# Half of each gated expert row split in SBUF and turned by DMA transposes, and the scaling of a quarter of the attention probabilities moved from ScalarE to GpSimd

## The reference, cut to what matters

```python
# attention, per sequence: q, k, v = x @ wq.T, ...; rope on q and k
w = jax.nn.softmax(jnp.einsum('bqh,bkh->bqk', q, k) / scale, axis=-1)
out = jnp.einsum('bqk,bkh->bqh', w, v)
...
for _ in range(LOOPS):                      # LOOPS = 2
    z_norm = _rmsnorm(z, norm_w)
    scores = jax.nn.softmax(z_norm @ router_w, axis=-1)
    topk_vals, topk_idx = jax.lax.top_k(scores, TOP_K)      # 2 of 8
    ...
    for e in range(E):                      # h = silu(x @ w1) * (x @ w3); h @ w2
        mixed = mixed + flat_cw[:, e:e + 1] * _swiglu(flat_z, w1[e], w3[e], w2[e])
    z = z + mixed.reshape(B, S, D)
```

## Time and profile before

| | |
|---|---|
| time, median of 3 runs | 1049.28 us (1046.91 to 1052.38) |
| the profiled execution | 1050.72 us, span 1049.0 us |
| granted TensorE clock | 0.989 |
| busy share of PE, DVE, ACT, POOL | 94%, 66%, 55%, 55% |
| instructions | 22711 |

### The profile page before, as it was taken

How to read it: one execution, slowest core, us unless ns; L and a number is a source line. 1 busy time by engine, 2 the same in 40 slices (tenths; PEclk the granted TensorE clock), 3 DMA queues, 4 the chain that set the end, 5 groups by cost and what they waited for, 6 DMA issues and landing times.

```text
span 1049.0 us, 22711 instructions
## 1 busy us (share of the span) xinstructions
PE 987.4 (94%) x7246; PEld 678.7 (65%) x7246; DVE 690.5 (66%) x1497; ACT 574.7 (55%) x1122; POOL 579.5 (55%) x755
## 2 busy tenths in 40 slices
PE   7999997989999899999999999999999999999991
PEld 5677776668888577665666765666755566666661
DVE  7889987999999454684435557535469433575557
ACT  4578786668888545433335565335574333333333
POOL 3356686866798755444443366443365544455435
PEclk9999999999999999999999999999999999999996
DMA  9921111000000234334346435338434433665573
GB/s 315 370 68 31 38 32 22 1 6 21 15 26 16 67 107 125 87 69 101 91 109 167 132 98 139 88 106 181 112 111 117 96 91 92 170 173 119 143 187 130
DMA packets 153818, 109.26 MB, mean 104 GB/s; under 512 B 100992, under 2 KB 140544, under 8 KB 153728
## 3 DMA queue, kind: packets, MB, share of 16 engines
q1 hardware_dynamic: 140096, 70.82, 26.5%
q0 software_dynamic: 13632, 37.24, 12.0%
HBM read 54.27 MB, written 31.20 MB: 81 GB/s over the span
## 4 chain that ended last, share of the span: by engine, by line
PE 69%; DVE 9%; POOL 7%; DMA 6%; ACT 4%; issue 3%; SPq 0%; another core or an unknown queue 0%; POOLq 0%; ACTq 0%; DVEq 0%
PE psum_s L930 32%; PE psum_o L2336 16%; PE psum_s L2325 6%; DMA arena<-arena 4%; PE psum_s L1758 3%; PE psum_t L1753 2%; PE psum_t L764 2%; PE psum_o L1804 2%; POOL arena L1057 2%; DVE arena L1489 1%; DMA arena<-in_rope 1%; PE psum_o L1799 1%; PE psum_o L1811 1%; PE psum_s L1735 1%; PE psum_t L2300 1%
## 5 line engine op out<-in xcount | busy, mean ns | idle before, releaser
L930 PE MATMUL psum_s<-w_all,arena 128*128 x1704 | 392.0, 380 | 4.6 <-issue 1.9
L1980 POOL DMA_INDIRECT token_rows<-arena,result_row_of_row x142 | 147.1, 1036 | 296.5 <-ACT arena L2089 291.2
L930 PEld LDWEIGHTS psum_s<-w_all,arena 128*128 128x128 f16 x1704 | 157.8, 98 | 185.2 <-issue 10.9
L2336 PE MATMUL psum_o<-w_all,arena 128*128 x1704 | 209.4, 273 | 9.1 <-DVE arena L2264 8.2
L915 DVE SCALAR_TENSOR_TENSOR arena<-psum_s,gate_scale,arena 128x512 f32<-128x512 f32 x142 | 106.5, 750 | 161.1 <-ACT arena L909 80.6
L2336 PEld LDWEIGHTS psum_o<-w_all,arena 128*128 128x128 f16 x1704 | 164.7, 98 | 54.1 <-issue 15.4
L2264 DVE TENSOR_TENSOR arena<-psum_s,arena 128x512 f16<-128x512 f32 x142 | 97.8, 689 | 132.3 <-ACT arena L2082 114.2
L2089 ACT ACTIVATE arena<-psum_o 128x256 f32<-128x256 f32 x142 | 54.3, 383 | 216.8 <-PE psum_o L2336 214.1
L891 POOL DMA_INDIRECT arena<-sorted_rows,token_of_row x142 | 139.9, 986 | 49.3 <-issue 40.2
L909 ACT ACTIVATE arena<-psum_s,silu_scale 128x512 f32<-128x512 f32 x142 | 97.6, 687 | 108.1 <-PE psum_s L930 56.6
L2082 ACT ACTIVATE arena<-psum_s 128x512 f16<-128x512 f32 x142 | 84.7, 597 | 33.1 <-PE psum_s L2325 22.9
(11 more groups left out here) (326 smaller groups left out, 1364.8 us busy)
## 6 DMA issues: line engine op xcount, KB each, us to landing
arena<-token_rows SPq DMA_DIRECT2D x64, 256.0 KB, 3.1
w_all<-in_L_ffn_w SPq DMA_DIRECT2D x24, 512.0 KB, 10.1
sorted_rows<-w_all SPq DMA_DIRECT2D x24, 256.0 KB
out<-x_sb SPq DMA_DIRECT2D x7, 512.0 KB, 3.1
arena<-arena SPq DMA_TRANSPOSE x172, 2.4
arena<-sorted_rows,token_of_row POOLq DMA_INDIRECT x142
token_rows<-arena,result_row_of_row POOLq DMA_INDIRECT x142
x_sb<-in_L_attn_x SPq DMA_DIRECT2D x1, 2048.0 KB, 14.8
```

The costliest lines, as they stand in the source:

```text
L930: last = nc.tensor.matmul(bank, e_xT[:, u, lx * DC + c, :], w_split[:, bass.ds(e * EW + at, FF)], start=(q == 0), stop=(q == 3 * DC - 1))
L1980: nc.gpsimd.indirect_dma_start(rows, bass.IndirectOffsetOnAxis(ap=targets[:, at : at + 1], axis=0), y_row[:, u, :], None).then_inc(s_sent[ ...
L2336: last = nc.tensor.matmul(psum_e, hT[:, lh, c, :], w_split[:, bass.ds(e * EW + at, D)], start=(q == 0), stop=(q == 3 * FC - 1))
```

## The change

It has two parts.

**Attention.** `quarter_hi` stands at the head of ScalarE's step, ahead of the copy of oT and of `p_copy(t-1, 1)`. The scaling of the quarter in place is no longer ScalarE's: GpSimd does it in `quarter_lo`, and then subtracts.

**Experts.** `turn_h` transposes only the first two of the four 128-column chunks, and `h_hi` and `h_lo` split only these. The other half of `h_row` is split in SBUF: `half_hi` on ScalarE (behind `beside`, ahead of `y_copy`) and `half_lo` on VectorE (right behind `gate`), each 128x256. SP turns the two with `turn_half`, two DMA transposes of 128x256 float16, ahead of everything else in its iteration. `outer` waits for them after its first six matmuls. To make room, `y_row` has two buffers and not three, `turn_rows` runs three tiles ahead, and `store_rows` is issued one iteration later.

```diff
+            if s:
+                dve.wait_ge(s_half_lo, s)          # in gate(s)
...
                 if l: sp.wait_ge(s_split_lo, t)
-                        sp.wait_ge(s_p_hi, 4 * t + 2)
+                        sp.wait_ge(s_quarter, t)
...
             def quarter_lo(t):
                 pool.wait_ge(s_quarter, t)
+                nc.gpsimd.tensor_scalar(probs[:, 0:512], probs[:, 0:512], P_SCALE, None, ALU.mult).then_inc(s_scaled, 1)
+                pool.wait_ge(s_scaled, t)
                 nc.gpsimd.tensor_tensor(probs_split[:, 1, :], probs[:, 0:512], probs_split[:, 0, :],
...
             def quarter_hi(t):
-                nc.scalar.activation(probs_split[:, 0, :], probs[:, 0:512], ACT.Copy, scale=P_SCALE).then_inc(s_p_hi, 1)
-                act.wait_ge(s_p_hi, 4 * t + 2)
-                nc.scalar.activation(probs[:, 0:512], probs[:, 0:512], ACT.Copy, scale=P_SCALE).then_inc(s_quarter, 1)
+                nc.scalar.activation(probs_split[:, 0, :], probs[:, 0:512], ACT.Copy, scale=P_SCALE).then_inc(s_quarter, 1)
...
+                if turn and quarter:
+                    quarter_hi(t - 1)              # head of step(t)
                 if turn and quarter:
-                    p_copy(t - 1, 1)
-                    quarter_hi(t - 1)
+                    p_copy(t - 1, 1, 2)
...
+            def turn_half(n):
+                for l, ready in enumerate((s_half_hi, s_half_lo)):
+                    sp.wait_ge(ready, n + 1)
+                    if n and l == 0:
+                        sp.wait_ge(s_e, n)
+                    sp.dma_start(hT[:, l, FC // 2 :, :], h_split[:, l, :], transpose=True).then_inc(s_half_T, 16)
             for k, plan in enumerate(plans):
                 for t in range(PASS[k]):
-                    turn_rows(sp, FIRST[k] + t + 2)
+                    n = FIRST[k] + t
+                    turn_half(n)
+                    if n == 0:
+                        turn_rows(sp, 2)
+                    turn_rows(sp, n + 3)
...
-                    if k < END and 0 <= t - plan.split - 1 < PAIRS:
-                        store_rows(k, t - plan.split - 1)
+                    if k < END and 0 <= t - plan.split - 2 < PAIRS:
+                        store_rows(k, t - plan.split - 2)
...
+            def half_hi(n):
+                act.wait_ge(s_h, n + 1)
+                if n:
+                    act.wait_ge(s_half_T, 32 * n)
+                nc.scalar.activation(h_split[:, 0, :], h_row[:, FF // 2 :], ACT.Copy).then_inc(s_half_hi, 1)
             def y_copy(n):
-                if n >= UNROLL:
-                    act.wait_ge(s_sent[u], 16 * (n // UNROLL))
+                if n >= 2:
+                    act.wait_ge(s_sent[(n - 2) % UNROLL], 16 * ((n - 2) // UNROLL + 1))
...
                     if k < END:
                         beside(k, plan, t)
+                    half_hi(n)
                     if n:
                         y_copy(n - 1)
...
+            def half_lo(n):
+                dve.wait_ge(s_half_hi, n + 1)
+                nc.vector.tensor_tensor(h_split[:, 1, :], h_row[:, FF // 2 :], h_split[:, 0, :], ALU.subtract).then_inc(s_half_lo, 1)
...
                     gate(dve, n)
+                    half_lo(n)
...
             def turn_h(n):
                 pe.wait_ge(s_h, n + 1)
-                for c in range(FC):
+                for c in range(FC // 2):
...
                 for q, (c, lh, lw) in enumerate([(c, a, w) for c in range(FC) for a, w in ((0, 0), (1, 0), (0, 1))]):
+                    if q == 3 * FC // 2:
+                        pe.wait_ge(s_half_T, 32 * (n + 1))
```

More of the change, by code:

```diff
@@ L305, in sandwich_kernel @@
         s_p_lo = sem("pT_lo")
-        s_quarter = sem("first_quarter_scaled")
+        s_quarter = sem("first_quarter_hi")
+        s_scaled = sem("first_quarter_scaled")
         s_split_lo = sem("first_quarter_lo")
@@ L798, in sandwich_kernel @@
         hT = take(2 * FF // 2).bitcast(F16).rearrange("p (l c t) -> p l c t", l=2, c=FC)
-        y_row = take(UNROLL * D).rearrange("p (u d) -> p u d", u=UNROLL)
+        y_row = take(2 * D).rearrange("p (u d) -> p u d", u=2)
+        h_split = take(FF // 2).bitcast(F16).rearrange("p (l c) -> p l c", l=2)
         z_early.append(take((NT - 2) * D))
@@ L830, in sandwich_kernel @@
         s_h_lo = sem("hT_lo")
+        s_half_hi = sem("h_second_half_hi")
+        s_half_lo = sem("h_second_half_lo")
+        s_half_T = sem("h_second_half_turned")
         s_e = sem("expert_out_ready")
@@ L1162, in qk_hi, with p_copy @@
                                      psum_t[1][:, :].rearrange("p (m t) -> p m t", m=2), ACT.Copy).then_inc(s_qk_hi, 1)
-            def p_copy(t, g):
+            def p_copy(t, g, count=1):
                 act.wait_ge(s_tp, 4 * t + g + 1)
                 out = pT[:, 0, g * 512 : (g + 1) * 512] if g < 2 else pT_whole[:, (g - 2) * 512 : (g - 1) * 512]
-                nc.scalar.activation(out, psum_t[g % 2][:, :], ACT.Copy, scale=P_SCALE).then_inc(s_p_hi, 1)
+                nc.scalar.activation(out, psum_t[g % 2][:, :], ACT.Copy, scale=P_SCALE).then_inc(s_p_hi, count)
             def quarter_hi(t):
@@ L1501, in p_lo @@
             def p_lo(t, g, first=False):
-                dve.wait_ge(s_p_hi, 4 * t + 1 if first else 4 * t + g + 1)
+                dve.wait_ge(s_p_hi, 4 * t + g + 1)
                 at = slice(g * 512, (g + 1) * 512)
@@ L1981, in send @@
                     rows, bass.IndirectOffsetOnAxis(ap=targets[:, at : at + 1], axis=0),
-                    y_row[:, u, :], None).then_inc(s_sent[u], 16)
+                    y_row[:, n % 2, :], None).then_inc(s_sent[u], 16)
             def last_root(q):
@@ L2081, in h_hi @@
                 act.wait_ge(s_th, s + 1)
-                nc.scalar.activation(hT[:, 0, :, :].rearrange("p c t -> p (c t)"), psum_h, ACT.Copy).then_inc(s_h_hi, 1)
+                nc.scalar.activation(hT[:, 0, 0 : FC // 2, :].rearrange("p c t -> p (c t)"), psum_h[:, 0 : FF // 2],
+                                     ACT.Copy).then_inc(s_h_hi, 1)
+            def half_hi(n):
[3 more added lines that the diff above has]
+                nc.scalar.activation(h_split[:, 0, :], h_row[:, FF // 2 :], ACT.Copy).then_inc(s_half_hi, 1)
             def y_copy(n):
-                u = n % UNROLL
                 act.wait_ge(s_e, n + 1)
-                if n >= UNROLL:
-                    act.wait_ge(s_sent[u], 16 * (n // UNROLL))
-                nc.scalar.activation(y_row[:, u, :], psum_e, ACT.Copy).then_inc(s_yrow, 1)
+                if n >= 2:
+                    act.wait_ge(s_sent[(n - 2) % UNROLL], 16 * ((n - 2) // UNROLL + 1))
+                nc.scalar.activation(y_row[:, n % 2, :], psum_e, ACT.Copy).then_inc(s_yrow, 1)
             for k, plan in enumerate(plans):
```

4 lines of the change are left out of this document (2 added, 2 removed).

## The result

The changed kernel takes **1234.67 us** (median of 4 runs, 1231.14 to 1242.73), the kernel before beside it 1048.85 (1046.91 to 1052.38): ratio 1.179, 95% interval 1.175 to 1.183. It is 186 us slower. The prediction was 1063, with a range up to 1085: right in direction, wrong by 172 us in size.

What follows compares the result with a forecast made beforehand. TensorE was taken to bound the kernel, busy 987.4 of 1049 us. Terms -32.7 + 13.2 + 12.3 + 5 + 7.5 + 5 + 3 + 0.4 gave +13.7 us, a median of 1063 us, range 1036 to 1085.

Steps and rivals of the forecast that it cites:

- 1: All expert tiles: two of four TensorE transposes go, 0.23 us in each of 142 tiles, -32.7 us if nothing else binds.
- 2: Plain expert tiles: a half transpose issues in 0.78 us, lands in 1.6; lo part 0.9 us early, no stall.
- rival C: Expert tiles: a half transpose costs what a whole one does, so plain tiles stall too; 1117 us, chance 0.08.
- 3: Row stretches: row_hi waits for stores in a 7.2 us loop; +13.2 and +12.3 us, +5 in pass 0.
- 4: Last pass's combine: loads queue behind half_lo's transpose, every second tile 2.5 us late over six tiles, +7.5 us.
- 5: VectorE where router work binds: its longer work costs some 8 tiles 0.6 us each, +5 us.
- 6: Start and two pass ends: the gather comes late, about 1 us each, +3 us.
- 7: First attention: each of 14 steps 0.1 us longer, last step's wait goes; +0.4 us, bounds -5 and +3.

Runs made afterwards that it cites:

- e4: Changed kernel with the two half transposes replaced by plain DMA copies of the same size, second half of hT left unturned: 1131.21 us.
- e5: e4 with TensorE reading the next tile's expert number between the two products of inner: 1120.46 us.
- e14: e13 with the early read of the next expert's number and the attention part as before the change: 1066.84 us.
- e7: Changed kernel with SP issuing store_rows at the head of its iteration, ahead of turn_half: 1187.33 us.
- e15: e14 with SP issuing the loads for combine ahead of turn_half: 1050.87 us, ratio 1.001 to 1.004.
- e16: e15 with half_lo on GpSimd, between its gather and scatter, instead of on VectorE: 1050.05 us, ratio 1.000 to 1.003.
- e2: Changed kernel with hi and lo turned by one 128x512 DMA transpose instead of two of 128x256: 1157.75 us.
- e8: Changed kernel with one transpose a tile, two buffers for split half and hT's second half, SP's other work mostly ahead of turn_half: 1110.82 us.
- e11: Changed kernel with one transpose a tile, store_rows first, outer one tile later, two hT buffers, one split-half buffer: 1106.39 us.
- e13: e11 with two buffers for the split half and one for y_row: 1085.63 us.

## Why the prediction was wrong, point by point

**1, -32.7 us for two transposes: wrong.** "If nothing else comes to bind" was the condition, and something did: the expert's number is read between the transposes and `inner`. Two transposes took 0.44 us to `inner` where four took 0.46. The term was 0 (e4: 70.07 for the 16 plain tiles, 69.92 before), and came in full only with the read moved, and then in single tiles (4.12 us in e5 and e14; over the 16 tiles 4.23 and 4.18). The row had shown nothing idle there because the transposes covered it; I named no cover for what I removed.

**2, the half transpose: the step that failed most.** I took the issue as 0.78 us, the fixed part and half of the rest; it has 1.23, no less than a transpose of twice the size. The landing I took as 1.6; the second transpose landed 3.7 and 3.9 us after its issue in the two cases shown, and 2.4 fits the tile of 4.60. And the hi transpose, which I had issued at 1.5 behind `outer`, closes a loop with `outer` that the working does not have. The estimate from the Trainium skill (page "DMA: Bandwidth & Descriptors", section "Why a DMA increments its semaphore by 16 and not by 1"), 0.82 by its count of crossbar tiles, fails in the same way: the runs have 1.23 for 128x256 beside 1.19 for 128x512, so here the issue does not grow with the tiles. My own sentence on the upper bounds (a landing at 5.1 against 4.78, a stall in each tile) was the case that came, and I gave it 0.08 as rival C. C's 1117 was too low as well: it kept the -32.7, had only a constant 0.4 us of stall, and let each long issue pass without effect. (Its 39 for 105 tiles is also not 5.1 less 4.78, which gives 34.) Plain tiles took 5.0 on average.

**3, the row stretches: right in mechanism, short in size.** `row_hi` waited 18 times for a store, six in each pass, 87.4 us in all. One turn of the loop in the chain that ended last, from issue to issue, is 8.74 us where I had 7.2:

```profile
682.99 1.18 SPq L1947
...
684.22 1.24 SPq L1947
...
685.55 1.22 SPq L908
...
686.82 2.86 DMA sorted_rows<-w_all
...
691.73 1.18 SPq L1947
```

For the six tiles I had said 43 us for passes 1 and 2 and 36 for pass 0, measured 49.75, 49.12 and 44.40. The terms that were mis-sized are the two issues (0.45 too low each) and the store's landing, 2.8 instead of 2.1 (with the attention part alone, e1, the median was 2.2). With them the sum is 8.8. e7 took the loop away, and 39 us in these 18 tiles, 47 in all.

**4, the last combine: right place, too small.** Six tiles were to take near 32 us; the 8 tiles took 51.66 where 34.94 stood before, +16.7. Loads behind the half transposes are a cause: putting them first brought the 8 tiles from 44.8 (e14) to 34.76 (e15). (The load's landing in the working adds up to 7.8, not 7.9.)

**5 and 6, VectorE and pass ends.** Not told apart. The wait of `outer` for `h_lo` grew from 8.2 us in 8 tiles to 61.0 in 26, so point 5 was probably too small as well, with part of it from the late loads of point 4. e16 took `half_lo` off VectorE and changed nothing measurable, but GpSimd may have taken the gain back, so the size of term 5 stays open.

**7, attention: +0.4, measured about +2.** Within its bounds, but not by the steps: `quarter_hi` of the tiles 1 to 15 runs from 58.8 to 164.8, 7.57 us a step as before. GpSimd's scaling takes 1.50 us. Where the 2 us arise was not looked into.

**The sum.** I treated the stretches as separate and each plain tile as having 0.9 us in hand. The 18 tiles of the row stretches and the 8 of the last combine hold 66 of the 186 us; the other 116 tiles lost about 1 us each, for which the sum had 8 us in all (points 5 and 6). With 1.23 for an issue and 2.4 and more for a landing the reserve was gone, and then every disturbance (a long issue, a store, a load, a gather) went through to TensorE. The runs put the loss at: number of issues (77 us by e2), transposes against plain copies (103, e4), store order (47), buffers (36); they overlap and are no sum.

## What to carry to other kernels

Before taking work from the busiest engine, ask what that work covers on the same engine: here the transposes covered a register read, and two of them removed gave nothing until the read was moved. A DMA of an unseen size should be costed at the nearest seen one, not by proportion, and an issue of a fixed price should be merged with its neighbour. A round trip over a DMA wants slack for its disturbed length, not its best one, and a second buffer at each of its ends. Here a path of 4.4 us was fitted into 4.8 (my estimate for one transpose a tile) and still stalled 35 times (e8); a whole tile of slack ended the stalls, and each single buffer that was left closed the loop again somewhere else (e11, e13).

## What the runs showed of the hardware

- The issue of a DMA transpose in SBUF took 1.23 us at 128x256 and 1.19 at 128x512 (medians); as plain copies of 128x256 the same two had 0.54 each. The issue of one and the same store of 256 KB took 0.36 us before the change and 0.57 after it, with plain copies too (0.57, e4).
- Some issues took twice as long (the half transposes up to 2.43 us). In the trace they stand beside 16 KB fetches of instructions: of the 35 transposes of the experts that took over 1.5 us to issue, 23 have such a fetch within the issue, of 40 ordinary ones drawn at random 1. This was seen, not tested.
- After a long wait TensorE was granted less clock. In the changed kernel it was idle for 4.40 us ahead of an `outer`; the 3.4 us behind were granted half clock (the lower of the two levels, 1.2 GHz), and that `outer` took 2.46 us instead of 1.47:

```profile
701.00:704.50 3.50, 0.34 (x4) 1.00 0.39 95
704.50:707.90 3.40, 3.40 (x16) 0.50 0.47 134
```

```profile
704.16 2.46 PE L2370 MATMUL psum_o<-w_all,arena 128*128 x12 [4.40 <-DVE arena L2291]
```

The mean clock was 0.957 (0.989 before), so some of the loss was lost twice. By my estimate that is (1 - 0.957) x 1229.4 - (1 - 0.989) x 1049.0 = 41 us at most.
